# Attention kernel: the next pair's query and key loads wait for the running unit's turned maxima

## What is computed

```python
qk = jnp.einsum('bceqd,bcekd->bceqk', q, k) / math.sqrt(h)
a = jax.nn.softmax(qk, axis=-1)
o = jnp.einsum('bceqk,bcekd->bceqd', a, v)
```

## Time and profile before

| what | value |
|---|---|
| median of three runs | 1186.38 us (1186.24 to 1190.86) |
| the profiled execution's own time | 1183.59 us |
| its span | 1181.8 us |
| TensorE (PE) busy | 1063.4 us, 90% |
| VectorE (DVE) busy | 838.1 us, 71% |
| GpSimd (POOL) busy | 746.7 us, 63% |
| ScalarE (ACT) busy | 695.4 us, 59% |

### The profile page before, as it was taken

One profiled execution on the slowest core, in us unless ns is written; L12 is line 12 of the kernel. 1 busy time (PEld: TensorE's weight loads), 2 busy tenths in 40 slices (PEclk: granted clock), 3 DMA queues, 4 the chain that ended last, 5 costly groups with the idle time before them and its releaser, 6 DMA issues. The chain is left out here.

```text
span 1181.8 us, 25543 instructions
## 1 busy us (share of the span) xinstructions
PE 1063.4 (90%) x10352; PEld 565.4 (48%) x10352; DVE 838.1 (71%) x1210; ACT 695.4 (59%) x1148; POOL 746.7 (63%) x770
## 2 busy tenths in 40 slices
PE   0899999999998987999999999999977799799997
PEld 0777777777772232333333333333323345454553
DVE  5888776666669985888888888888832675544344
ACT  3866677777651664666666666666655332446345
POOL 1144455555552986888888888889867319909900
PEclk9999999999996998999999999999989899999999
DMA  9934424432464845264455555361050699766661
GB/s 306 308 104 129 131 75 139 133 108 67 115 155 138 119 132 92 56 100 88 75 91 91 99 100 89 70 99 58 11 161 19 227 333 294 225 233 161 201 205 47
DMA packets 137765, 159.05 MB, mean 135 GB/s; under 512 B 17856, under 2 KB 85712, under 8 KB 137644
## 3 DMA queue, kind: packets, MB, share of 16 engines
q1 hardware_dynamic: 114544, 122.58, 42.6%
q10 hardware_dynamic: 14560, 25.66, 6.4%
q0 software_dynamic: 8544, 9.18, 3.0%
HBM read 106.54 MB, written 52.89 MB: 135 GB/s over the span
## 5 line engine op out<-in xcount | busy, mean ns | idle before, releaser
L1289 POOL TENSOR_TENSOR a_pl<-a_prob 128x512 bf16<-128x512 f32 x416 | 450.5, 1108 | 84.7 <-ACT a_prob L1246 82.2
L1246 ACT ACTIVATE a_prob<-a_col 128x512 f32<-128x512 f32 x512 | 288.4, 596 | 166.1 <-PE a_col L1157 160.7
L1205 DVE TENSOR_REDUCE a_negmax<-a_row 128x1 f32<-128x512 f32 x384 | 244.8, 679 | 50.6 <-PE a_row L1136 50.5
L522 PE MATMUL f_acc<-f_wh,f_xhl 128*32 128x384 bf16 x2560 | 163.5, 327 | 1.0 <-DVE f_yl L640 1.0
L1216 DVE TENSOR_TENSOR a_pl<-a_prob 128x512 bf16<-128x512 f32 x96 | 121.2, 1262 | 25.1 <-ACT a_prob L1246 25.1
L1157 PE MATMUL a_col<-a_q,a_k 98*128 98x512 bf16 x256 | 98.7, 393 | 34.5 <-ACT a_prob L1246 19.8
L640 DVE TENSOR_TENSOR f_yl<-f_acc,f_yh 128x768 bf16<-128x768 f32 x80 | 75.3, 955 | 75.6 <-ACT f_yh L754 75.6
L877 POOL TENSOR_TENSOR f_straight<-f_straight,f_turned 128x832 f32<-128x832 f32 x40 | 85.4, 2135 | 60.1 <-DVE f_turned L666 60.1
L1157 PE MATMUL a_col<-q,k 98*128 98x512 bf16 x256 | 100.2, 391 | 15.6 <-ACT a_prob L1246 13.7
L522 PE MATMUL f_acc<-f_wl,f_xhl 128*32 128x384 bf16 x1280 | 107.9, 326 | 0.0
L1575 PE MATMUL b_acc_s<-b_xh,b_mat_h 128*104 128x512 bf16 x256 | 98.8, 386 | 10.1 <-DVE b_xl L1659 9.0
(11 more groups left out here) (177 smaller groups left out, 2045.9 us busy)
## 6 DMA issues: line engine op xcount, KB each, us to landing
X<-b_x ACTq DMA_DIRECT2D x16, 526.0 KB, 8.5
a_v<-V SPq DMA_DIRECT2D x16, 512.0 KB, 4.7
Z<-a_z ACTq DMA_DIRECT2D x32, 256.0 KB, 6.1
b_res<-X SPq DMA_DIRECT2D x38, 208.0 KB
out<-b_y ACTq DMA_DIRECT2D x38, 208.0 KB
V<-f_vout SPq DMA_DIRECT2D x64, 104.0 KB
b_raw<-X SPq DMA_DIRECT2D x24, 258.0 KB, 7.3
q<-in_x SPq DMA_DIRECT2D x6, 1024.0 KB, 5.9
```

Of the source, the lines that this page charges most:

```text
L522: last = nc.tensor.matmul(acc[half][c * KW:(c + 1) * KW, part, 0:PART], xx[g % 2][:, (half * QUAD + c) * FH + f, at], ww[half * QUAD + c][ ...
L1205: nc.vector.reduce_max(negmax[n % PAIR][:, 0, t:t + 1], row[step % ROWS][:], AX.X, negate=True).then_inc(max_done, 1)
L1246: nc.scalar.activation(prob[sets_done % RING][:, t % QUAD, :], col[step % 2][:], ACT.Exp).then_inc(exp_done, 1)
L1289: nc.gpsimd.tensor_tensor(pl[p][:, r, :], prob[p][:, r, :], ph[p][:, r, :], ALU.subtract).then_inc(lo_pool, 1)
```

## The change

`m` is the unit whose maxima are asked for: 4(i-1)+2 for the entry-0 tiles of pair i, 4i for the entry-1 tiles. Part 0 of each load now waits until the maxima of unit m have landed. For pair 0 nothing changes: the only such load, of entry 1, waited for `max_in[0]` at 16 before and does so after. So six places get a new wait: entries 0 and 1 of pairs 1, 2 and 3 (m = 2, 4, 6, 8, 10, 12).

```diff
             def load_qk(i, s, part):
-                if i == part == 0:
-                    sp.wait_ge(max_in[0], 16)
+                if part == 0:
+                    m = PAIR * (i - 1) + CHANNELS * (s + 1)
+                    sp.wait_ge(max_in[m % PAIR], 16 * (m // PAIR + 1))
                 if i:
                     sp.wait_ge(col_full, STEPS * (PAIR * (i - 1) + CHANNELS * (s + 1)) - (1 - part) * QT * HALF)
                 load_rows(sp, QK, q[s], 0, i, s, part, qk_in[s][part])
```

## The result

The changed kernel takes 1174.62 us (median of 9 runs, 1170.63 to 1178.77); the kernel before, timed beside it, 1185.65 us (9 runs, 1178.80 to 1190.86). The ratio is 0.9905, 95% interval 0.9884 to 0.9925: faster by about 1%, or 11 us. The forecast was 1176.0 us, faster by 10.4. A control of the same kernel in a later set gave 0.9904 (0.9881 to 0.9926).

The account below looks back on a forecast made before the run. PE, busy for 90% of the span, was the nearest thing to a bound. Terms: 10.67 - 0.3 + 0 = 10.4 us, so 1186.4 - 10.4 = 1176.0 us, chance 0.80, range 1173 to 1181.

Parts of the forecast that it names:

- Place and size of the stall: Attention stage, interval between maxima transfers of units 2 and 3: 42.90 us against a beat of 32.23, so 10.67 us lost.
- The residual of 0.3 us: Stall expected to remain at unit 2 after the change, bounds 0 and 0.9 us, leaving a gain of 10.4 us.
- their 3.95 us: Time unit 2's maxima may take from issue without stopping PE, 437.71 to 441.66; they took about 13 us.
- The lower bound: Residual stall of 0 at unit 2: the maxima's trip runs beside earlier traffic and lands by 441.0, before 441.66.
- rival (a): Unit 2: side, centre and output transfer still hold the maxima; gain only 6.8 to 8.4 us, 1178 to 1179.6; chance 0.10.
- The restart at half clock: After unit 2's stall PE restarted at 0.50 of its clock, costing 1.56 us beyond the 9.11 idle; this should go too.
- Rival (b): Unit 2: query and key transfers do not delay the maxima, since queues take turns; gain 0, time 1186.4 us; chance 0.05.
- 8.1 against 2.6 us: Landing time of a 256 KB output transfer on ACT's queue, issued while the 12 loads move against near their end.
- The five other waits at 0: Moving part 0 at m = 4, 8, 12 and at m = 6, 10 was taken to cost 0 us.
- rival (c): Part 0 meets V load and part 1, delaying units 5, 9, 13; up to 1208 us; 0.02, beyond 0.5% slower 0.03.
- the prediction's worst case: At m = 4, 8, 12: train ends at 548.8, maxima land at 552.1, PE waits 3.0 us, 4.6 with slow restart, three times.
- `blend` moves up whole: Stage after attention has nothing that ran beside the stall, so it starts earlier by the full gain; span 1181.8 to 1171.4.

Follow-up runs that it names:

- the kernel with both waits: Changed kernel, with loads of `blend`'s first tiles also waiting for unit 15's maxima; 1162.12 us, ratio 0.9801 to the kernel before; second run 1166.83 us, 0.9846.
- six transfers in front: Kernel before, with only the six key transfers of pair 1's entry-0 part 0 waiting for unit 2's maxima; 1181.99 us, ratio 0.9961.
- the run with V ahead of part 0: Changed kernel, with the V load issued ahead of entry 1's part 0 for pairs 1 to 3; 1188.46 us, ratio 1.0013 to the kernel before.

## Why the prediction was right, and where it was off

- **Place and size of the stall.** Right. 10.67 us were to be lost at unit 2 and nowhere else that the change touches; the interval fell by 42.90 - 32.22 = 10.68, and the wait of unit 2 alone gives the whole ratio. The total is a weaker test: 11.0 us measured against 10.4 forecast, with an interval of about 2.4 us to either side.
- **The residual of 0.3 us.** It was 0. Side, centre and the output transfer stayed ahead of the maxima, but PE does not show a wait, so the maxima landed within their 3.95 us: SP, released by them, went on at 440.36, 2.6 us after their issue. The lower bound was the true one, and rival (a) did not happen.
- **The restart at half clock.** Right, but the earlier trace rows show the clock at 0.50 only while PE stands still. These stretches of the kernel before show it after the restart at 450.77:

```profile
450.77:452.00 1.23, 1.23 (x6) 0.25 (x10) 0.18 (x1) 0.55 (x1) 0.00 (x0) 0.50 0.00 0
453.00:454.00 1.00, 1.00 (x13) 0.16 (x6) 0.00 (x0) 0.00 (x0) 0.17 (x1) 0.50 0.00 0
455.00:456.00 1.00, 0.97 (x5) 0.23 (x4) 1.00 (x3) 1.00 (x3) 0.84 (x1) 1.00 0.00 0
```

  With the stall gone the clock of the interval rose from 0.88 to 1.00, and the gain contains the 1.56 us beyond the idle time.
- **Rival (b), the load is not what delays the maxima.** It did not happen: the wait grows with the transfers that SP issued first, 0, 3.81 and 9.11 us for none, six and twelve. The evidence of the earlier trace rows, 8.1 against 2.6 us, is stronger than the prediction had it. The first of these two output transfers was issued at 534.58, and from 535 to 540 no packet of ACT's queue moved at all; this is the only queue that did:

```profile
q1 hardware_dynamic: 478, 0.70, 106.2%
```

  The rival was argued from the Trainium skill, "DMA: Bandwidth & Descriptors", section "Queues, rings and completion order", by which an engine changes between its queue rows after each packet. What failed here is the step from that rule to a small transfer that lands nearly as when alone. Whether the rule itself failed is open: the section counts typically 9 to 17 descriptors to a packet. From 535 to 540 each of the 16 engines moved on average 30 of the profile's packets for SP, and the profile does not tell how many of these make one turn. Nor does it tell whether ACT's transfer stood ready in its queue all that time.
- **The five other waits at 0.** Right, by the kernel that has them alone. The train of loads was forecast to end at 545 on the old time axis, 10.6 us ahead of the new one, thus 534.4; it ended between 533 and 534. The point from which rival (c) costs, given as 546.5, is 549.06 - 3.3 = 545.8 by the trip of 3.3 us that the prediction's worst case uses; the train stayed short of either.
- **`blend` moves up whole.** This step was off by 1.4 us in the profiled pair. Attention's last stretch took 54.47 in place of 53.72 us and `blend` 261.51 in place of 260.85, so the span fell by 9.2 where 10.4 was forecast. The same kernel differs by as much between executions (the changed kernel's second profile has 53.97 and 261.00, the kernel with both waits 256.80 and 264.45 for `blend`), and the medians, 11.0 us apart, do not show a loss.

## What to carry to other kernels

A transfer of a few KB on which the busiest engine waits (here 16 KB) should not be issued behind a bulk load (here 0.8 or 1.6 MB) that will still be moving when the engine needs it, even if it has a queue of its own; let the load wait for it, or start the load early enough. Look for where in a repeating list the load slips out of phase, such as behind one-off constants: that is the one place to mend. The move has a far edge too: with part 0 of entry 1 another 10 us later, the loads hit the next unit's maxima, and 9.4 us were lost there.

## What the runs showed of the hardware

- A 16 KB transfer on ACT's queue moved no packet for 3 us while twelve 128 KB transfers on SP's queue were moving, and a 256 KB transfer none for 5 us. Both queues had work issued to them; one of them moved. Just before, from 437 to 442 us, both had moved, 421 packets of SP's and the 144 of an output transfer that ACT had issued ahead of the twelve. So the order was close to the order of issue; what makes it so was not measured.
- A late transfer of 16 KB cost more than the engine's idle time: 10.67 us for 9.11 at unit 2, and 5.9 for 3.81 with six transfers in front (38.10 - 32.23). The surplus is PE at half its clock (1.2 GHz) for 3 to 4 us after the restart. In the run with V ahead of part 0, a wait of 2.25 us left the clock at 1.00 (the interval of 34.52 us), and one of 3.29 us did not (37.58 us, clock 0.91).
- At unit 15 the surplus is larger and varies: 7.2 us for 4.5 before, 8.0 for 3.9 after, 11.7 for 3.67 with six transfers in front. There PE ran at half clock for about 9, 9 and 12 us after the restart, and in the last two profiles the clock had already been at half for some 3 us before the wait began. So the price of a stall cannot be read from its length alone.
- The same kernel, timed in two sets on two chips, gave 0.9801 (0.9776 to 0.9826) and 0.9846 (0.9824 to 0.9869): the intervals barely overlap. An interval from one set understates what a repeat can give.
